# Neighbour product ahead of the aggregation, self product inside attention, layer norm of the gnn in three groups

## The chip, the cores and the metric

One core of one Trainium2 chip runs the kernel. The metric is the device time of one execution in microseconds (us). Before the change three runs took 770.51, 771.01 and 771.20 us, median 771.01. The engines are PE (matrix products, into the eight banks of PSUM), DVE (vector), ACT (scalar), POOL (GpSimd) and SP, which here only issues DMAs. Each engine takes its instructions in the order in which they were written; engines wait for one another by semaphores.

## The reference

1250 nodes of 512 numbers, 40,000 edges sorted by destination.

```python
xn = layernorm(x)
# gnn
agg = segment_sum(xn[src], dst) / max(count, 1)
h   = xn @ w_self.T + agg @ w_neigh.T + bias
gnn = relu(layernorm(h) * gamma + beta)
# linear attention, 8 heads of 64; phi(t) = elu(t @ proj_mat) + 1
q, k, v = split(xn @ w_qkv)
mix = ((phi(q) @ (phi(k).T @ v)) / (phi(q) @ sum(phi(k)))) @ w_proj + b_proj
x = x + gnn + mix
# feed-forward: shared and 8 routed experts (2 of one group of 4 for each node)
y = layernorm(x) * ln_scale + ln_bias
x = x + shared(y) + sum of two weighted expert outputs(y)
```

## The kernel before

All rows live on chip as ten tiles of 125 nodes. Every product with weights is split: both operands are a high and a low float16 half, and three of the four combinations are summed, so that one tile times one 512x512 matrix is 4 x 3 = 12 matmuls (`split3`, L1291). A "unit" is a weight block of 128x2048 floats: SP loads it into one of two staging buffers (L283), ACT writes its high half scaled by 256 (L423), DVE its low half (L733), into one of eight slots.

The stages, in PE's order, are these.

1. Prologue. The rows are normalised by tiles (`stats`, `scale_rows`), transposed (`turn_x`) and split (`xT_high` on ACT, `xT_low` on DVE). Key weights are folded with the projection matrix (`fold`, `wp_high`, `wp_low`). Then come key products (`keys_mm`; ACT's relu and exp, DVE's `key_sum`) and value products (`values_mm`), and their sum over nodes (`kvacc`). Beside it ACT writes the high halves of the rows (`rows_high`) and POOL the low halves (`rows_low`, L339) for the aggregation. DVE then works out from the sorted edges where each block of destinations begins (L830 to L874).
2. Counting and aggregation, 45 rounds. DVE writes one-hot matrices of a round (L885, L888) into a ring of four buffers, PE counts edges by product (L1325) and, one block of 125 destinations later, sums the sources' rows with these counts (`spread`, L1337). Key and value products and folds are put between rounds at fixed places (`KEY_AT`, `VAL_AT`, `FOLD_AT`).
3. Query stage. DVE divides the ten blocks of sums by the counts (L981); PE transposes them (`means_T`, L1481) among the twelve query products, ACT and DVE split them (L562, L985). Query features are relu and exp on ACT, a sum on DVE (L996).
4. Attention. For each tile PE has `att` (16 small products, L1509), `att_turn` of the tile before (four transposes, L1518), and `project` of the one before that (12 matmuls). DVE divides (L1010, L1017), ACT and DVE split the transposed tile (L586, L1022), DVE adds the projection to x (`mix_add`, L1028), POOL has added b_proj (L348). Banks of `att` alternate.
5. gnn. For each tile PE has a bias product (L1302), 12 matmuls of the self weights and 12 of the neighbour weights with the transposed means into one bank. ACT copies it out (L592). DVE has statistics, scale and shift in groups of 4, 4 and 2 tiles (`gnn_norm`), adds to x and norms again (`ffn_norm`), PE transposes the result (`yT`, L1551), ACT applies ln_scale and ln_bias (L600) and both split it (L603, L1097).
6. Hidden layer of the experts, `hid_e`, 48 matmuls a tile in four banks; ACT has silu (L611) and a store (L615), DVE the product (L1106). The `yT` of groups 1 and 2 stand in pairs between halves of tiles. At tile 4 the router's small products stand between the others. Then come the shared layer, the routed experts and the output.

## Time and profile before

| | us |
|---|---|
| median of three runs | 771.01 |
| the profiled execution | 768.86 |
| its span, first to last instruction | 767.0 |
| PE busy in the span | 728.9 (95%) |
| DVE busy | 410.6 (54%) |
| ACT busy | 262.2 (34%) |
| POOL busy | 172.3 (22%) |
| PE's share of the chain of waits | 75% |

The numbers of the last section come from the profiled execution, with times counted from the start of its span. A matmul's own duration in the trace overlaps with the next one, so what a group of matmuls costs is read from the distance between the starts of groups, or from the chain of waits, which gives each piece only its own time.

### The profile page before, as it was taken

The numbers are of one execution on the slowest core, as the hardware profiler recorded it, in microseconds if no ns is written. First come the engines' busy times: TensorE is split into PE (matmuls) and PEld (weight loads), VectorE is DVE, ScalarE is ACT, GpSimd is POOL, SyncE is SP. The second block draws the span as 40 slices with busy tenths as digits, with TensorE's granted clock in tenths as the row PEclk, the third lists the DMA queues.
The fourth block names the chain that finished last, engine by engine and source line by source line (L and its number), as shares of the span: only waits on it lengthen the run. The fifth ranks groups of instructions, "written<-read, shape, count | busy, mean of one in ns | idle before, by whom it ended". The sixth has DMA issues, their size and how long they took to land.

```text
span 767.0 us, 12139 instructions
## 1 busy us (share of the span) xinstructions
PE 728.9 (95%) x4376; PEld 449.7 (59%) x4376; DVE 410.6 (54%) x805; ACT 262.2 (34%) x386; POOL 172.3 (22%) x167
## 2 busy tenths in 40 slices
PE   6989999999799999989999999999889999999998
PEld 5645677776466655656665654445744555555554
DVE  5978977894466768687435432222254524421064
ACT  3852222221483222325634223333353624422000
POOL 3340000000016000002212237742221222211363
PEclk9999999999999999999999999999999999999999
DMA  9200003000021133001144312113167766443675
GB/s 238 97 1 1 1 1 111 1 1 14 1 81 58 56 114 106 1 1 43 47 136 124 93 48 57 43 32 99 51 246 255 279 232 232 128 132 126 201 204 163
DMA packets 24418, 73.91 MB, mean 96 GB/s; under 512 B 7059, under 2 KB 7405, under 8 KB 20274
## 3 DMA queue, kind: packets, MB, share of 16 engines
q1 hardware_dynamic: 8607, 39.74, 15.4%
q0 software_dynamic: 10768, 25.52, 11.5%
q10 hardware_dynamic: 4994, 8.01, 2.9%
q8 instruction: 31, 0.51, 0.3%
q14 instruction: 18, 0.14, 0.1%
HBM read 57.90 MB, written 15.31 MB: 95 GB/s over the span
## 4 chain that ended last, share of the span: by engine, by line
PE 75%; DVE 11%; ACT 6%; issue 3%; DMA 3%; DVEq 0%; POOL 0%; ACTq 0%; SPq 0%; POOLq 0%
PE banks L1295 55%; PE banks L1337 6%; PE banks L1325 6%; PE banks L1638 2%; DMA y_rows<-xT 1%; DVE st L756 1%; ACT W L423 1%; DVE W L733 1%; PE banks L1509 1%; PE banks L1318 1%; DMA x<-in_x 1%; DMA stg<-in_units 1%; PE banks L1518 1%; DVE xn L1106 1%; ACT big L600 1%
## 5 line engine op out<-in xcount | busy, mean ns | idle before, releaser
L1295 PE MATMUL banks<-W,xT 128*125 128x512 f16 (+1 forms) x1392 | 318.0, 383 | 10.0 <-ACT xT L698 4.4
L1295 PEld LDWEIGHTS banks<-W,xT 128*125 128x125 f16 (+2 forms) x1392 | 165.2, 122 | 139.2 <-issue 18.1
L1295 PE MATMUL banks<-xT,W 128*128 128x500 f16 (+1 forms) x720 | 129.8, 342 | 1.8 <-DVE xn L1245 1.4
L1295 PEld LDWEIGHTS banks<-xT,W 128*128 128x128 f16 x720 | 70.3, 98 | 59.5 <-issue 2.8
L733 DVE SCALAR_TENSOR_TENSOR W<-stg,W 128x2048 f16<-128x2048 f32 x30 | 68.2, 2290 | 44.4 <-ACT W L423 44.4
L1295 PE MATMUL banks<-W,big 128*125 128x512 f16 x360 | 81.5, 380 | 0.0
L1295 PEld LDWEIGHTS banks<-W,big 128*125 128x125 f16 x360 | 48.3, 136 | 29.2 <-issue 2.3
L365 POOL DMA_INDIRECT xn<-h_rows,tokidx x29 | 35.4, 1221 | 128.3 <-PE banks L1638 118.5
L1265 DVE CAST xT<-banks 128x1024 f32 x22 | 26.9, 1222 | 69.2 <-PE banks L1638 69.2
L354 POOL TENSOR_TENSOR big<-xn,big 125x512 f16<-125x512 f32 x20 | 23.4, 1172 | 176.4 <-ACT big L615 176.4
L423 ACT ACTIVATE W<-stg 128x2048 f16<-128x2048 f32 x30 | 56.5, 1904 | 3.9 <-DMA stg<-in_units 3.9
L348 POOL TENSOR_TENSOR x<-x,bproj 125x512 f32<-125x512 f32 x10 | 14.4, 1478 | 181.9 <-DVE big L996 181.9
L1337 PE MATMUL banks<-W,big 125*125 125x512 f16 x200 | 54.0, 393 | 0.6 <-ACT big L554 0.6
L1245 DVE SCALAR_TENSOR_TENSOR xn<-banks,xn 128x500 f32<-128x500 f32 (+1 forms) x24 | 14.2, 591 | 69.8 <-ACT xn L677 69.8
L698 ACT ACTIVATE xT<-banks 128x512 f32<-128x512 f32 x23 | 13.7, 596 | 66.8 <-PE banks L1295 50.6
L378 POOL TENSOR_TENSOR big<-xn,big 128x500 f16<-128x500 f32 (+1 forms) x24 | 22.7, 945 | 46.0 <-ACT big L680 46.0
L885 DVE TENSOR_TENSOR W<-big 125x2000 f16<-125x2000 f16 x26 | 31.1, 1197 | 3.3 <-DVE big L880 3.2
L522 ACT ACTIVATE big<-banks 128x500 f16<-128x500 f32 (+1 forms) x27 | 14.2, 527 | 49.2 <-PE banks L1325 49.2
L677 ACT ACTIVATE xn<-banks 128x500 f32<-128x500 f32 (+1 forms) x24 | 12.4, 516 | 52.7 <-PE banks L1295 47.6
L1106 DVE SCALAR_TENSOR_TENSOR xn<-banks,xn 125x512 f32<-125x512 f32 x20 | 13.8, 689 | 30.6 <-ACT xn L611 30.5
L1638 PEld LDWEIGHTS banks<-ident,xn 128*128 (+1 forms) x384 | 24.0, 100 | 8.5 <-issue 1.8
L1638 PE MATMUL banks<-ident,xn 128*128 128x128 f16 x384 | 26.2, 223 | 2.9 <-POOLq L370 1.5
(289 smaller groups left out, 856.1 us busy)
## 6 DMA issues: line engine op xcount, KB each, us to landing
stg<-in_units SPq DMA_DIRECT2D x30, 1024.0 KB
y_rows<-xT ACTq DMA_DIRECT2D x29, 256.0 KB
h_rows<-big POOLq DMA_DIRECT2D x10, 500.0 KB, 3.6
out_x<-x SPq DMA_DIRECT2D x10, 224.0 KB
stg<-in_wqkT SPq DMA_DIRECT2D x2, 1024.0 KB, 11.9
x<-in_x SPq DMA_DIRECT2D x2, 896.0 KB
xn<-h_rows,tokidx POOLq DMA_INDIRECT x29, 4.5
x<-in_x SPq DMA_DIRECT2D x1, 448.0 KB
```

Source lines behind the costliest of these rows:

```text
L354: g.tensor_tensor(hrow[t % 2][:, HID + 512 * u:HID + 512 * (u + 1)], mscr[0:P, 1024 + 512 * u:1536 + 512 * u], hrow[t % 2][:, 512 * u:512 ...
L365: g.indirect_dma_start(hg[i % 2], None, h_rows, bass.IndirectOffsetOnAxis(ap=tokidx[:, i:i + 1], axis=0)).then_inc(g_in[i % 2], 16)
L378: g.tensor_tensor(hT[:, 1, j, c0:c0 + w], mscr[:, 1024 + 512 * (n % 2):1024 + 512 * (n % 2) + w], hT[:, 0, j, c0:c0 + w], ALU.subtract).th ...
L423: s.activation(W[:, u % NSLOT, 0, :], stg[:, u % NSTG, :], ACT.Copy, scale=WS).then_inc(S["w_h"], 1)
L733: v.scalar_tensor_tensor(out=W[:, u % NSLOT, 1, :], in0=stg[:, u % NSTG, :], scalar=WS, in1=W[:, u % NSLOT, 0, :], op0=ALU.mult, op1=ALU.s ...
L885: v.tensor_tensor(oht[z % RING], iotaK.unsqueeze(1).to_broadcast(wide), krel[k].rearrange("p (a b) -> p a b", b=2).unsqueeze(2).to_broadca ...
L1106: v.scalar_tensor_tensor(out=mscr[0:P, 1024 + 512 * u:1536 + 512 * u], in0=ps[2 * u + 1][0:P, :], scalar=HS / WS, in1=mscr[0:P, 512 * u:51 ...
L1265: v.tensor_copy(hgT[:, bass.ds((i + 1) % 2, 1), 1].rearrange("p z j n -> p (z j) n"), turned[1]).then_inc(S["hg_l"], 1)
L1295: ins = te.matmul(dst, lhs(sl, c), rhs(sr, c), start=(first and c == 0 and k == 0), stop=(last and c == n - 1 and k == 2))
L1325: ins = te.matmul(ps[q][:, h * KEYS:(h + 1) * KEYS], ohp[z][:, a, :, b], oht[z][:, a, :, b], start=(a == 0 and b == 0), stop=(a == CH // 2 ...
L1337: ins = te.matmul(ps[4 + z][0:BLK, :], CT[z][0:P, t, :], xs[:, s, t, :], start=(t == 0 and s == 0), stop=(t == TILES - 1 and s == 1))
L1638: ins = te.matmul(turned[s][:, j, :], rows(s * HID + j * 128), ident16[:, :], start=True, stop=True)
```

## The change

The aggregation is linear, so agg @ w_neigh.T is the sum of the rows (xn @ w_neigh.T)[src], divided by the count. The changed kernel computes that product for every source row in the prologue, and the aggregation sums its results.

- w_neigh is no unit any more. SP loads it raw right behind the first two tiles of x (x now comes in groups of 2, 4 and 4 tiles, the key weights behind them); ACT and DVE split it in four pieces each (`wn_high`, `wn_low`). `neigh_mm(t)` is 12 matmuls; ACT (`yn_high`) and DVE (`yn_low`) split its result straight from PSUM into what `spread` reads. `rows_high` and POOL's `rows_low` are gone.
- Five key products and one value product now stand ahead of the rounds, where nine and four stood; the others are between the rounds, at changed places.
- Division, `means_T` and their splits are gone from the query stage. It has two unit conversions and `bias_rows`. POOL's additions of b_proj start at its beginning, where they began after it.
- The self product stands in the attention loop between `att` and `att_turn` of the same tile; its bank and the sums, times the reciprocal count, are combined by DVE (`combine`), with the first statistics. `att` has two banks instead of four.
- The gnn layer norm goes in groups of 3, 3 and 4 tiles, the first of them in the attention loop; the transposes of each group stand together, four in a row. The router's small products are at tile 5.

The core of the diff:

```diff
-KEY_AT = {3: 9}
-VAL_AT = {1: 4, 5: 5, 10: 6, 16: 7, 22: 8, 28: 9}
-FOLD_AT = {12: 4, 15: 5, 18: 6, 21: 7}
+KEY_AT = {1: 5, 4: 6, 7: 7, 10: 8, 13: 9}
+VAL_AT = {2: 1, 5: 2, 8: 3, 11: 4, 16: 5, 20: 6, 24: 7, 28: 8, 32: 9}
+FOLD_AT = {17: 4, 21: 5, 25: 6, 29: 7}
+XG = [(0, 2), (2, 4), (6, 4)]
+LG = [(0, 3), (3, 3), (6, 4)]
...
 # ACT, after the query stage
+            for t in range(TILES):
+                if t == 3:
+                    sqrts(*LG[0])
+                if t == 6:
+                    sqrts(*LG[0])
+                    sqrts(*LG[0])
+                act.wait_ge(S["tT_mm"], t + 1)
...
+                s.activation(attT(t)[:, 0], ps[6 + t % 2][:, 0:C * P]...
+                if t < 3:
+                    unit(U_EIN + t)
+                if t == 7:
+                    for n in range(C):
+                        yT_high(n)
+                if t == 8:
+                    unit(U_EIN + 3)
...
+            hid_e(0)
+            hid_e(1, (0,))
+            sqrts(*LG[1])
+            sqrts(*LG[1])
+            hid_e(1, (1,))
+            for n in range(C, 2 * C):
+                yT_high(n)
+            sqrts(*LG[2])
+            hid_e(2)
+            hid_e(3, (0,))
+            sqrts(*LG[2])
+            sqrts(*LG[2])
+            hid_e(3, (1,))
+            hid_e(4, (0,))
+            for n in range(2 * C, 3 * C):
+                yT_high(n)
+            hid_e(4, (1,))
...
 # DVE
+            def yn_low(t):
+                dve.wait_ge(S["xs_h"], t + 1)
+                v.scalar_tensor_tensor(out=xs[:, 1, t, :], in0=ps[4 + t % 2][0:P, :], scalar=HS / WS, in1=xs[:, 0, t, :], op0=ALU.mult,
+                                       op1=ALU.subtract).then_inc(S["xs_l"], 1)
...
+            def combine(t):
+                dve.wait_ge(S["gn_mm"], t + 1)
+                link(v.scalar_tensor_tensor(out=h[:, t, :], in0=h[:, t, :], scalar=cntacc[:, t:t + 1], in1=ps[2 + t % 2][0:P, :],
+                                            op0=ALU.mult, op1=ALU.add))
+                v.bn_stats(st[:, t, :], h[:, t, :]).then_inc(S["gn_add"], 1)
...
+            for t in range(TILES):
+                att(t)
+                if t >= 2:
+                    mix_add(t - 2)
+                if t < 3:
+                    unit(U_EIN + t)
+                if t == 3:
+                    gnn_rsqrt(*LG[0])
+                if t == 4:
+                    gnn_scale(*LG[0])
+                if t == 5:
+                    ffn_add(*LG[0])
+                if t == 6:
+                    ffn_norm(*LG[0])
+                if t == 8:
+                    for n in range(C):
+                        yT_low(n)
+                if t == 9:
+                    unit(U_EIN + 3)
+                combine(t)
+                attT_low(t)
...
+            ffn_norm(*LG[2])
+            hid_e(3, (1,))
+            late_constants()
+            hid_e(4, (0,))
+            for n in range(2 * C, 3 * C):
+                yT_low(n)
...
 # PE, prologue
             turn_x(0)
             turn_x(1)
+            neigh_mm(0)
+            neigh_mm(1)
+            turn_x(2)
+            turn_x(3)
...
             fold(0, ps[2])
             fold(1, ps[7])
+            neigh_mm(2)
+            turn_x(4)
...
 # PE, attention
+            for t in range(TILES + 1):
+                if t < TILES:
+                    att(t)
+                    self_mm(t)
+                    att_turn(t)
+                if t >= 1:
+                    project(t - 1)
+                if t == 7:
+                    for n in range(C):
+                        if n == 1:
+                            pe.wait_ge(S["tT_rdy"], 8)
+                        yT(n)
...
             hid_e(0)
-            yT(4)
-            yT(5)
-            hid_e(1, (0,))
-            yT(6)
-            yT(7)
-            hid_e(1, (1,))
+            hid_e(1)
+            for n in range(C, 2 * C):
+                yT(n)
             hid_e(2)
...
+            hid_e(3)
+            hid_e(4, (0,))
+            for n in range(2 * C, 3 * C):
+                yT(n)
+            hid_e(4, (1,))
```

## Rows read from the trace of the kernel before

**Rows 1.** Busy time by stretch: length, then each engine, PEclk, DMA share, GB/s.

```profile
0.00:62.66 62.66, 51.77 (x312) 36.61 (x313) 45.63 (x110) 34.58 (x61) 19.93 (x33) 1.00 0.37 103
62.66:188.92 126.26, 123.11 (x935) 89.58 (x934) 101.92 (x214) 29.25 (x53) 0.00 (x0) 1.00 0.06 20
188.92:225.99 37.07, 31.83 (x187) 18.70 (x186) 20.23 (x38) 21.28 (x43) 0.00 (x0) 0.95 0.09 29
225.99:329.62 103.63, 102.24 (x588) 65.47 (x587) 71.96 (x158) 30.99 (x44) 14.40 (x10) 0.98 0.20 67
329.62:378.10 48.48, 44.86 (x217) 28.54 (x218) 31.71 (x85) 24.24 (x40) 10.26 (x10) 1.00 0.12 33
```

**Rows 2.** Waits of PE: total, times, longest.

```profile
PE banks L1481 <- DVE big L985: 5.2, 2, 3.2
```

**Rows 3.** The chain of waits: start, own time, piece.

```profile
93.07 2.59 PE banks L1295 x12
...
206.56 0.86 PE banks L1481 x8
```

**Rows 4.** Timeline of the prologue and first rounds: start, duration, instruction, idle time before.

```profile
15.48 0.69 DVE L777 SCALAR_TENSOR_TENSOR W<-banks,W 128x512 f16<-128x512 f32 x1
...
42.74 0.65 DVE L830 TENSOR_REDUCE big<-big 80x4 f32<-80x500 int32 x1 [2.18 <-issue]
...
44.99 1.06 DVE L836 CAST big<-big 80x4 f32<-80x4 int32 x1
...
46.09 0.19 DVE L837 CAST etabs<-etabs 125x50 f32<-125x50 int32 x1
...
57.19 1.20 DVE L885 TENSOR_TENSOR W<-big 125x2000 f16<-125x2000 f16 x1 [0.49 <-DVE big L880]
...
76.46 1.07 PE L1325 MATMUL banks<-W 125*128 125x250 f16 x8
```

**Rows 5.** Timeline of attention.

```profile
227.89 14.40 POOL L348 TENSOR_TENSOR x<-x,bproj 125x512 f32<-125x512 f32 x10 [181.86 <-DVE big L996]
...
232.01 1.90 ACT L423 ACTIVATE W<-stg 128x2048 f16<-128x2048 f32 x1
...
233.95 2.29 DVE L733 SCALAR_TENSOR_TENSOR W<-stg,W 128x2048 f16<-128x2048 f32 x1 [1.12 <-ACT W L423]
...
243.61 1.09 PE L1509 MATMUL banks<-kvbd,big 64*125 64x65 f32 x16
...
244.97 0.76 DVE L1017 TENSOR_TENSOR xn<-banks,rs 125x256 f32<-125x256 f32 x2
...
247.80 1.09 PE L1509 MATMUL banks<-kvbd,big 64*125 64x65 f32 x16
```

**Rows 6.** Timeline of the gnn products, the bias product of two tiles.

```profile
276.01 0.42 PE L1302 MATMUL banks<-rows,ones 2*125 2x512 f16 x1
...
281.69 0.42 PE L1302 MATMUL banks<-rows,ones 2*125 2x512 f16 x1
```

**Rows 7.** Timeline of the norms of group 0 (four tiles).

```profile
294.91 0.17 DVE L741 TENSOR_SCALAR rs<-mv 125x4 f32<-125x4 f32 x1
...
296.36 2.74 DVE L1067 SCALAR_TENSOR_TENSOR xn<-xn,mv,gcat 125x512 f32<-125x512 f32 x4
...
304.44 2.47 DVE L756 BATCH_NORM_STATS2 st<-x 125x6 f32<-125x512 f32 x4
```

**Rows 8.** Two stretches of 12 and 12 matmuls, and that of the late constants, by engine.

```profile
196.08:200.31 4.23, 4.23 (x15) 1.68 (x13) 0.68 (x1) 0.59 (x1) 0.00 (x0) 0.60 0.00 0
231.49:235.30 3.81, 3.81 (x15) 1.93 (x13) 2.20 (x3) 2.38 (x2) 3.81 (x4) 0.69 0.00 0
271.16:274.01 2.85, 2.85 (x15) 1.82 (x14) 2.67 (x8) 0.00 (x0) 0.00 (x0) 1.00 0.00 0
```

**Rows 9.** Timeline of the hidden layer, ACT.

```profile
338.73 1.28 ACT L611 ACT_TABLE_LOAD   x1
...
344.70 0.75 ACT L600 ACTIVATE big<-banks,lnsb 128x500 f32<-128x500 f32 x1
```

488 lines of the change are left out of this document (200 added, 288 removed).

## The prediction

> **What bounds the kernel now.** I read the summary first: the tensor engine (PE) is busy 95% of the span and is most of the chain of waits, so the question of each edit is what work it takes from PE and what idle time it opens or closes there. I then cut the span at the kernel's own stages [rows 1]. Prologue, first row: PE is busy 51.8 of 62.7 us. Counting and aggregation, second row: 123.1 of 126.3. The query stage, third row: 31.8 of 37.1, with a granted clock of 0.95. Attention and the gnn products, fourth row: 102.2 of 103.6. The hidden layer up to its fifth tile, fifth row: 44.9 of 48.5. The whole edit lies before 378 us; behind it nothing changes but that everything comes earlier or later. The list of waits shows that PE's longest wait inside a stage is for the vector engine (DVE) and its low half of the transposed means, 5.2 us in two waits, one of 3.2 [rows 2].
>
> **Work that is removed.** Ten transposed means leave PE: eight transposes took 0.86 us [rows 3], 40 take 4.3. The neighbour product itself is only moved: 12 matmuls are 2.59 us [rows 3], ten tiles 25.9. The self product, its bias rows and the feed-forward transposes stay.
>
> **Query stage.** Without means nothing stands between the twelve query products. Eight of them are 500 wide (2.54 us each by the same column rate as 2.59 for 512) and four 250 wide (1.3): 25.5 us. ACT needs about 1.45 us for one, so PE keeps the pace. The new attention wants all twelve banks released where it wanted the tenth: about 0.9 us behind the last product. So 26.4 where 37.07 were [rows 1]: 10.7 less, of which 4.3 is the work above and 6.4 idle time, slow clock included (range 5 to 7). What is late next is nothing of this stage; the two unit conversions in it lie beside PE work.
>
> **Prologue and the first rounds.** The neighbour product needs its weight split and x transposed, and its result is evacuated and split: one more ACT step (about 0.6) and one more DVE step (0.69) a tile, by the like split of the folded weights [rows 4]; bounds 0.5, a split from SBUF in a unit, and 0.9. I walk DVE's queue. First rows at about 5.5 (an estimate for half the bytes; anything up to the end of the warm-up matmuls at 12.1, less 4 us of statistics, is hidden), both halves of the weight by 16.0, so the first product starts at 16.0 with 2.8 us of idle PE before it. Then statistics, inverse root and scaling of tiles 2 to 5 (2.5+0.4+1.45+1.9), statistics of tiles 6 to 9 (2.5), two splits of products and two of x: the third product can start at 26.8, PE having run dry at 24.1. Tile 4's start at 34.7 is PE's own pace, and so are the rest: the tenth ends at 52.2, its split at 53.8. There DVE begins the index block, which began at 42.74 [rows 4]: 11.1 later. That block took 14.45 to the first one-hot [rows 4]; it now has one more key sum (0.7) and a wait for PE (0.4). Two tiny casts in it took 0.95 and 1.06 us, while GpSimd was busy with the subtractions that the change drops; I take back 1.7 (bounds 0 and 1.7, from the 0.19 of the like cast right behind, in the same group). So the one-hots of round 0 start at 67.5 and its count at 69.9, against 62.66, where the second stage begins [rows 1]. In the first five rounds DVE sets the pace again: masks and table lie between the one-hots, and the fifth count comes at 86.0 against 76.46 [rows 4]. Up to there PE did three more products and three fewer key-value sums (7.8-1.35 = 6.4), so 3.1 us of the 9.5 is new idle; 0.9 comes back in round 5, where PE waited for DVE and now has a key product to do. From there the rounds are full of PE work as before, with six products more. Net: 2.2 us of idle added (range -2, if the loads come sooner and the pieces fit, to +6).
>
> *What the skill adds.* The Trainium skill (SBUF — State Buffer, "Who interferes with whom") says that GpSimd and DVE share one port pair as an exclusive lock, for casts and for DVE operations with two inputs in SBUF. The long cast agrees. By the rule the 1.7 us is certain; without it the sum would be 1.7 higher. The rule also speaks against the change, which moves GpSimd's ten bias additions beside the query sums; but a unit split with two SBUF inputs took its usual 2.29 us beside those additions [rows 5], and DVE has some 10 us to spare in that stage.
>
> **Attention with the self product.** One tile of attention was 4.19 us of PE (from one group of products to the next) [rows 5]. Half a gnn tile is added: 5.68 us for 24 matmuls and the bias [rows 6], so 2.59 + 0.36 + 0.14 = 3.09. Ten tiles of 7.28 are 72.8, 12 transposes for the layer norm 1.4. Against that stands the order of the queues. For t = 0, 1, 2 ACT converts a unit (1.90 us [rows 5]) behind its evacuation of the transposed attention, and DVE's split of that unit (2.29) stands ahead of combine(t), attT_low(t) and att(t+1), for which PE waits before the next transposes. From the end of PE's att(0): self 3.05, transposes 0.5, evacuation 0.8, unit 1.9, its split 2.3, combine 1.4 (a 0.69 and a 0.68 operation), low half 0.65, att(1) 0.95 (its two products 0.76 [rows 5], reciprocals ahead): 11.6. PE is through with att(1) and self(1) at 7.6. It waits 4.0 us. In the next two tiles the same loop is 8.6 against PE's 7.2: 1.4 each. Then group 0 of the norms: 1.45 for an inverse root, 4.1 for scale and shift of three tiles, 4.0 for add and statistics, 4.9 for the second norm (two roots, three small steps, three scalings of about 0.5) [rows 7]. DVE's base is 3.75 a tile, so it falls behind in t = 4 to 6 and PE waits 1.1 in t = 7. The four transposes at t = 7 share two banks with ACT behind them: 1.2, and 0.15 at the last projection. Sum: 72.8+1.4+6.8+1.1+1.35 = 83.5; walked through, the pieces overlap and it is 82.6. PE's clock fell to 0.60 right behind the 3.2 us wait and to 0.69 near the start of attention [rows 8]; behind the 4.0 us wait I expect the same, most of it in the shadow of the next waits, and none at the start, since dense products now follow att(0) at once: 0.7 more, 83.3. With 25.9 of neighbour product gone from 103.6, 77.7 would be even: 5.5 too many (range 2 to 9; the low end if the unit loop overlaps where I made it serial).
>
> **Hidden layer.** Before, transposes went in pairs between the halves of a tile. Now four stand in a row, twice. Group 1, in time from the start of tile 0: PE ends tile 1 at 20.8. DVE adds group 1 behind tile 0 (12.0 to 16.1), multiplies tile 1's first half at 17.2, and then has the second norm with two roots that ACT must answer, the first behind a table load of 1.28 [rows 9]: rows ready at 23.5. Two transposes, then the third waits for ACT, which has another table load, a silu and its store first: tile 2 starts at 26.8 where 22.2 would do. 4.6 idle. Group 2: rows are ready in time (52.7 against 52.8), but behind the first two transposes stand ACT's table load, silu and store of tile 3, then tile 4's first half, for which DVE first does the late constants (2.85 us [rows 8]), then the affine evacuation of 0.75 [rows 9]. PE goes on at 60.1, 7.3 later, for 1.8 of work: 5.5 idle. Together 10.1 against 4.4 before (48.48 less 4 x 10.37 of products and 2.6 of transposes); with 0.65 of transposes more, 6.35 too many (range 2 to 9). In the second gap PE stands still for 4.7 us, longer than the 3.2 that cost a slow clock [rows 2, 8]; twelve matmuls there took 4.23 instead of 2.54 [rows 8], so 1.7 on top (0 to 3.5 with the first gap and the prologue's). Routing has 32 us of PE cover left where it had 42 and needs 25: nothing.
>
> **Sum.** -4.3 -6.4 +2.2 +5.5 +6.35 +1.7 = +5.05 us. The profiled execution was 768.86 us (span 767.0), so 773.9; the median of the runs is 771.01, 0.28% higher. On that base: 776.
>
> **Rivals.** *A, faster: DVE's queue does not hold up PE in attention and the hidden layer.* One mechanism: the order in which conversion, combine and low half are queued. For it: DVE is busy only 72.0 of 103.6 us there now [rows 1], so that it has room on the average. Against it: the loop is serial, by the order of the code, and each piece has its row. Price: without the 6.8 and 5.7 us and the 1.7 of clock the sum is -9.1, 762; if only the 6.8 fall away, 769. It decides once these two stages have under some 10 us of new waits where I count 15. *B, no change:* the prologue fits (its 2.2 falls away) and the clock costs nothing: +1.2, 772. For it: both are the least certain terms. *C, worse:* the prologue's two dry spells (2.8 and 2.7) each bring a slow clock, the weight lands late, and the hidden layer's first gap too is followed by a slow clock: +3 and +3, 782.
>
> **Chances.** My forecast 0.40 (773 to 779), C 0.15, B 0.17, A 0.28, of which most near 769. A measurement can tell 0.2%, 1.5 us, from no change. A's upper edge and B's lower lie about that bound, so faster 0.30, same 0.16, slower 0.54. Range 764 to 783; the likeliest case alone 773 to 779.
>
> **What would show it.** The query stage at 26 us without a clock dip (else the 10.7 is wrong). First count near 70. In attention, PE waits before its transposes of about 4, 1.4, 1.4 us for DVE at t = 1 to 3. In the hidden layer waits of transposes for ACT, the longest near 4.7, behind it a granted clock below 1. If the attention waits are under 2 us in all, rival A holds; if the first count comes behind 75, rival C.

## The result, and the profile after

The changed kernel takes 789.25 us (median of four runs, 785.72 to 794.09) where the kernel before took 771.11 beside it: ratio 1.0247, 95% interval 1.0194 to 1.0300. Slower, as forecast, but by 18 us where I said 5, and outside the range of 764 to 783. Its profiled execution took 788.64 us, span 786.8.

The same stretches as in [rows 1], from the profile after, in the same columns (the sixth is the whole tail, from the transposes of the first expert rows on; the 164.27 us between the fifth and the sixth are the same in every profile within 0.03):

```profile
0.00:68.10 68.10, 57.38 (x300) 39.64 (x301) 47.94 (x122) 28.92 (x49) 5.76 (x23) 0.97 0.41 110
68.10:218.33 150.23, 147.15 (x1067) 103.48 (x1066) 107.49 (x222) 38.23 (x70) 0.00 (x0) 0.98 0.05 17
218.33:247.12 28.79, 25.55 (x148) 13.93 (x146) 18.56 (x24) 19.40 (x38) 16.15 (x10) 1.00 0.29 92
247.12:332.51 85.39, 79.60 (x462) 51.15 (x463) 60.41 (x141) 20.61 (x28) 0.00 (x0) 0.92 0.15 49
332.51:405.31 72.80, 61.51 (x271) 38.46 (x270) 45.83 (x107) 29.06 (x46) 13.86 (x13) 0.91 0.11 30
569.58:786.80 217.22, 205.85 (x1186) 110.58 (x1186) 82.74 (x74) 63.58 (x61) 57.74 (x48) 0.98 0.58 194
```

Set against the forecast's own path, stage by stage (us). "First count" is PE's first counting product, with which the rounds begin. The forecast's end of the rounds, 217.0, is their end before (188.92) with the moved neighbour product (25.9) and 2.2 of new idle time:

| stretch | forecast | measured | miss |
|---|---|---|---|
| to the first count | 69.9 | 68.10 | -1.8 |
| rounds (to 217.0, less 69.9) | 147.1 | 150.23 | +3.1 |
| query stage | 26.4 | 28.79 | +2.4 |
| attention | 83.3 | 85.39 | +2.1 |
| hidden layer, against before | +8.05 | +13.7 | +5.7 |
| tail (214.05 before) | 0 | 217.22 | +3.2 |
| sum | +5.05 | +19.8 | +14.7 |

(The hidden layer now runs to tile 5 where [rows 1] end at tile 4: 72.80 less one tile of 10.37 is 62.4, against 48.7 from 329.62 to the like product.)

The column to read first is the last but two, the granted clock. It was below 1 in one stage of [rows 1] that matters, 0.95; now it is 0.92 and 0.91 in attention and the hidden layer. Cut at the places where it fell, it is 0.50, the lower of its two levels (1.2 of 2.4 GHz). Such a piece is called a slow stretch here:

```profile
15.68:19.09 3.41, 3.41 (x10) 1.79 (x8) 2.90 (x14) 0.80 (x2) 0.00 (x0) 0.50 1.07 214
77.12:83.95 6.83, 6.83 (x15) 2.67 (x15) 4.49 (x12) 0.00 (x0) 0.00 (x0) 0.50 0.01 1
247.79:254.61 6.82, 6.82 (x24) 3.90 (x22) 0.97 (x4) 0.00 (x0) 0.00 (x0) 0.50 0.00 0
261.44:268.27 6.83, 5.63 (x16) 3.37 (x16) 3.23 (x6) 2.38 (x2) 0.00 (x0) 0.50 0.36 144
357.01:363.84 6.83, 5.96 (x21) 3.63 (x20) 3.08 (x11) 6.39 (x11) 1.71 (x2) 0.50 0.29 76
394.56:401.39 6.83, 4.86 (x15) 3.20 (x16) 2.94 (x5) 5.74 (x9) 1.16 (x1) 0.50 0.17 51
```

PE is busy 33.5 of these 37.6 us and does half as much as it could: at most 16.8 us are lost. The kernel before had two such stretches of 3.4 us up to the same place. And the waits of PE in the whole kernel (total, times, longest), against [rows 2]:

```profile
PE banks L1542 <- ACT xn L572: 7.5, 6, 5.3
PE banks L1297 <- ACT xT L669: 6.2, 3, 4.5
...
PE banks L1542 <- DVE big L1070: 4.9, 2, 3.3
PE banks L1519 <- DVE xn L1005: 4.7, 3, 3.5
PE banks L1508 <- issue: 3.2, 1, 3.2
PE banks L1297 <- DVE W L760: 2.8, 1, 2.8
PE banks L1327 <- DVE W L877: 2.2, 1, 2.2
```

Each wait that I had named is there: L1519 the transposes of attention, L1542 those of the layer norm, L1297 <- L760 the first neighbour product. L1508, the first attention product, was forecast at 0.9 and is 3.2.

### The profile page after: what moved, and what is told of

Read it like the earlier page. It is cut to its first block, busy times and chain, and to the rows that moved or that the text cites. A ratio compares the mean times of both kernels' runs of the same rounds, so it can differ in the third digit from the quotient of the medians.

```text
span 786.8 us, 12045 instructions
## 1 busy us (share of the span) xinstructions
PE 737.1 (94%) x4336; PEld 451.5 (57%) x4336; DVE 417.8 (53%) x814; ACT 255.7 (32%) x372; POOL 160.3 (20%) x157
## 4 chain that ended last, share of the span: by engine, by line
PE 66%; DVE 14%; DMA 8%; ACT 5%; issue 4%; POOL 1%; ACTq 0%; DVEq 0%; SPq 0%; POOLq 0%
PE banks L1297 48%; PE banks L1339 6%; PE banks L1327 6%; DMA xT<-y_rows,sloti 3%; PE banks L1635 2%; DMA y_rows<-xT 2%; DVE W L703 2%; ACT W L416 2%; DMA x<-in_x 1%; DVE st L726 1%; POOL xT L401 1%; DVE x L1058 1%; DMA stg<-in_units 1%; DVE xn L1108 1%; PE banks L1320 1%
## 5 line engine op out<-in xcount | busy, mean ns | idle before, releaser
L1297 PE MATMUL banks<-W,xT 128*125 128x512 f16 (+1 forms) x1512 | 355.2, 390 | 10.3 <-ACT xT L669 6.2
L1297 PEld LDWEIGHTS banks<-W,xT 128*125 128x125 f16 (+2 forms) x1512 | 186.3, 126 | 155.0 <-issue 29.2
L1297 PE MATMUL banks<-xT,W 128*128 128x500 f16 (+1 forms) x720 | 127.4, 339 | 1.8 <-DVE xn L1247 1.4
L1297 PEld LDWEIGHTS banks<-xT,W 128*128 128x128 f16 x720 | 69.9, 97 | 59.2 <-DVE xn L1247 1.6
L347 POOL TENSOR_TENSOR xn<-xn 125x512 f16<-125x512 f32 x20 | 24.2, 1209 | 198.4 <-ACT xn L605 198.4
L341 POOL TENSOR_TENSOR x<-x,bproj 125x512 f32<-125x512 f32 x10 | 16.1, 1648 | 213.2 <-DVE tab L966 213.2
L416 ACT ACTIVATE W<-stg 128x2048 f16<-128x2048 f32 x29 | 54.5, 1901 | 4.5 <-DMA stg<-in_units 4.5
L1297 PE MATMUL banks<-W,big 128*125 128x512 f16 x240 | 53.9, 381 | 0.0
L1297 PEld LDWEIGHTS banks<-W,big 128*125 128x125 f16 x240 | 31.9, 136 | 19.7 <-issue 2.3
L669 ACT ACTIVATE xT<-banks 128x512 f32<-128x512 f32 x23 | 13.7, 596 | 69.0 <-PE banks L1297 51.8
L874 DVE TENSOR_TENSOR W<-big 125x2000 f16<-125x2000 f16 x24 | 28.8, 1199 | 4.0 <-DVE big L869 3.7
L1297 PE MATMUL banks<-W,xn 128*125 128x512 f16 x120 | 29.7, 402 | 0.0
L648 ACT ACTIVATE xn<-banks 128x500 f32<-128x500 f32 (+1 forms) x24 | 12.4, 516 | 52.7 <-PE banks L1297 47.5
```

Of the source, the lines that this page charges most:

```text
L347: g.tensor_tensor(hrow[t % 2][:, HID + 512 * u:HID + 512 * (u + 1)], mscr[0:P, 1024 + 512 * u:1536 + 512 * u], hrow[t % 2][:, 512 * u:512 ...
L416: s.activation(W[:, u % NSLOT, 0, :], stg[:, u % NSTG, :], ACT.Copy, scale=WS).then_inc(S["w_h"], 1)
L874: v.tensor_tensor(oht[z % RING], iotaK.unsqueeze(1).to_broadcast(wide), krel[k].rearrange("p (a b) -> p a b", b=2).unsqueeze(2).to_broadca ...
L1297: ins = te.matmul(dst, lhs(sl, c), rhs(sr, c), start=(first and c == 0 and k == 0), stop=(last and c == n - 1 and k == 2))
```

## The experiments

Two theories were tested. Theory 1, the clock: most of the miss is slow stretches behind dry spells of PE (idle time between its products), each dearer and more frequent than I priced them. Theory 2, the queues: the waits themselves were sized too low. In the table all stages are from one profile each (us). "Slow" lists the lengths of the slow stretches in the rounds, attention and the hidden layer; the tail is the rest from the experts' first turned rows.

| kernel | first count | rounds | query | attention | hidden | tail | slow |
|---|---|---|---|---|---|---|---|
| changed | 68.10 | 150.23 | 28.79 | 85.39 | 72.80 | 217.2 | 6.8 / 6.8, 6.8 / 6.8, 6.8 |
| e9, again | 69.25 | 148.58 | 28.77 | 85.41 | 72.51 | 217.1 | 3.4 / 6.8, 3.4 / 6.8, 6.8 |
| e1 fill | 69.70 | 151.80 | 28.76 | 82.74 | 68.90 | 213.5 | 10.2 / 3.4, 3.4 / none |
| e2 units | 69.27 | 148.59 | 28.77 | 79.02 | 72.49 | 217.5 | 3.4 / 6.8 / 6.8, 6.8 |
| e3 pairs | 72.18 | 150.23 | 28.77 | 82.69 | 62.77 | 218.8 | 6.8 / 3.4, 3.4 / 3.4 |
| e4 adds | 73.74 | 150.22 | 28.24 | 83.07 | 72.81 | 219.4 | 6.8 / 3.4, 3.4 / 6.8, 6.8 |
| e5 bias | 71.11 | 150.23 | 27.30 | 83.39 | 72.87 | 219.7 | 6.8 / 6.8 / 6.8, 10.2 |
| e6 folds | 79.37 | 150.22 | 28.77 | 82.71 | 72.73 | 217.5 | 6.8 / 3.4, 3.4 / 6.8, 6.8 |
| e12 no low | 69.18 | 150.19 | 28.77 | 85.27 | 69.48 | 218.3 | 6.8 / 6.8, 6.8 / 6.8, 6.8 |
| e15 order | 75.55 | 147.08 | 28.76 | 83.84 | 72.75 | 219.2 | none / 6.8, 3.4 / 6.8, 6.8 |
| e7 four | 80.76 | 148.54 | 27.31 | 77.63 | 62.67 | 219.9 | 3.4 / 3.4 / none |
| e10 three | 69.12 | 147.08 | 27.29 | 79.11 | 62.63 | 220.5 | none / 3.4, 3.4 / none |
| e11 + fill | 76.85 | 147.08 | 27.30 | 76.92 | 62.62 | 215.1 | none / none / none |
| e13 banks | 70.67 | 151.77 | 25.62 | 79.51 | 62.63 | 217.4 | 10.2 / 3.4 / none |
| e14 + fill | 72.41 | 147.10 | 25.62 | 79.46 | 62.64 | 214.9 | none / 3.4 / none |
| e16 best | 71.12 | 147.07 | 25.64 | 75.91 | 62.63 | 215.0 | none / none / none |

The column of the rounds is a measurement of the clock by itself. The code of the rounds is the same in all but e11, e14 and e16 (nine idle products there), and the stage takes 147.08 us with no slow stretch, 148.5 to 148.6 with one of 3.4, 150.2 with 6.8, 151.8 with 10.2: 1.5 to 1.7 us for each 3.4. In attention a stretch costs less: e7, e10 and e11 have the same code there and take 77.63, 79.11 and 76.92 us with 3.4, 6.8 and none, so 0.7 to 1.1 for each 3.4.

The tail, whose code no experiment touches, lies between 213.5 and 220.5 us in these profiles. A difference of a few us between two totals is therefore read from the stages.

### e1: products that nobody reads, in the hidden layer's dry spells

`fill(k)` is k products of 512 columns whose result is never used.

```diff
...
             hid_e(1)
+            pe.wait_ge(S["pr_add"], TILES)
+            fill(14)
             for n in range(C, 2 * C):
...
             for n in range(2 * C, 3 * C):
+                if n == 2 * C + 2:
+                    fill(24)
                 yT(n)
```

> The changed kernel with products that nobody reads, put where the tensor engine stands still in the hidden layer: 14 of 512 columns ahead of group 1's transposes (3.0 us in a wait of 3.3) and 24 between group 2's second and third set (5.2 us in a wait of 5.5). The order and the waits of the other engines stay. Theory 1 (the clock: each dry spell is followed by 6.8 us at 1.2 GHz, which costs 3.4 us): both slow stretches of the stage go, and from its first product to tile 5 it takes 66.1 us where the changed kernel took 72.9; the whole is some 6.8 us below the changed kernel, 782. Theory 2 (queues: the waits themselves are what I sized too low, and the clock falls whatever the engine does): the stage stays at 72.9 or is a little longer, and the whole stays near 789.

787.24 us (781.71 to 788.14), ratio 1.0223 (1.0159 to 1.0288). The total alone shows no clear gain over the changed kernel (1.0247). The profile below is of the fastest of the five executions, at a mean clock of 0.985; the other four, 786.29 to 788.14, had 0.978 and have no trace of their own, so where their slow stretches lay is not known. The stage, at a granted clock of 1.00:

```profile
333.00:401.90 68.90, 64.61 (x308) 40.75 (x307) 45.80 (x107) 29.06 (x46) 13.88 (x13) 1.00 0.12 32
```

Both slow stretches are gone and 3.9 us with them, not 6.8: from the last product of tile 1 to the first of tile 2 it is still 7.0 us (7.35 before), around group 2 10.1 (10.5). A slow stretch costs only what PE would have done in it on the path; about half of these lay in the waits. So in this profile theory 1 holds, at 3.9 for two where it had 6.8, and 13.7 less 3.9 is still 9.8 us of waits and transposes, where I had 6.35: theory 2 has a share too.

### e2: the unit conversions behind the low half

```diff
 # ACT, attention loop
-                if t < 3:
-                    unit(U_EIN + t)
+                if 1 <= t <= 3:
+                    unit(U_EIN + t - 1)
...
 # DVE, attention loop
-                if t < 3:
-                    unit(U_EIN + t)
...
                 combine(t)
                 attT_low(t)
+                if 1 <= t <= 3:
+                    unit(U_EIN + t - 1)
```

> The changed kernel with the three unit conversions of the attention loop one tile later on ACT (t = 1 to 3 for 0 to 2) and, on DVE, behind the low half of the transposed attention instead of ahead of the combination. If the serial loop through conversion and split is what holds the tensor engine (the prediction's step): the waits of 3.9, 1.4 and 1.4 us before the transposes shrink under 1 us together, the slow stretch behind the first of them goes (3.4), and the attention stage is 76 to 79 us where it was 85.4; the whole some 7 us below the changed kernel, 782. Rival (DVE has no room in these tiles whatever the order, with 3.75 us of base work and 2.3 of conversion in 7.3): the waits move to t = 2 to 4 and the stage stays at 83 to 85 us.

783.29 us (781.95 to 785.09), ratio 1.0180 (1.0115 to 1.0244). Attention 79.02 instead of 85.4. Its waits:

```profile
PE banks L1508 <- issue: 3.2, 1, 3.2
PE banks L1519 <- DVE xn L1005: 1.2, 2, 0.9
PE banks L1542 <- ACT xn L572: 1.1, 2, 0.6
```

3.5 of the 4.7 us at L1519 and the second slow stretch are gone, 6.4 together. The prediction's mechanism is right: the serial loop is what held PE.

### e3: the transposes in pairs

Group 1's first pair stands between the two banks of tile 2's first half, the second pair behind it; group 2's pairs stand around tile 4's second half; the late constants go ahead of the hidden layer.

> The changed kernel with the feed-forward transposes of groups 1 and 2 taken in pairs with two or more products of the hidden layer between them, as before the change (ACT's and DVE's evacuations follow in the same places), and DVE's late constants ahead of the hidden layer. Theory 1 (four in a row against two banks make the dry spells, and the clock falls behind them): both waits shrink under 1.5 us and both slow stretches go; from the first product to tile 5 some 63 to 65 us where it was 72.9, the whole near 781. Theory 2 (what holds is DVE's norm of a group, not the rhythm of the transposes): the waits for the rows stay (3.3 us ahead of group 1) and one slow stretch with them: 69 us, the whole near 785.

782.12 us (779.52 to 783.12), ratio 1.0152 (1.0085 to 1.0219). The hidden layer is 62.77, ten less, though one wait of 4.8 us for DVE's product came up towards tile 4, because I had put scale and add of group 2 in one piece. With the inverse root moved ahead of tile 2 (e7, e10) the stage still takes 62.6 us: the wait is split into several of 1.6 to 1.8. Four in a row against two banks was the larger fault. Of the ten us a part is the clock, since this profile has 3.4 us of slow stretches in the stage where the changed kernel has 13.7.

### e4 and e5: what holds PE ahead of attention

The core of the two edits:

```diff
 # e4, POOL
-            pool.wait_ge(S["ring_free"], 1)
+            pool.wait_ge(S["q_rdy"], 3 * PAIRS)
 # e5, DVE: bias_rows() behind att(0); PE, self_mm(0)
-                add_bias(d)
-                split3(d, xl(t), unitv(U_SELF), C, False, True)
+                split3(d, xl(t), unitv(U_SELF), C, True, False)
+                pe.wait_ge(S["b_rdy"], 1)
+                te.matmul(d, ones16[0:2, 0:P], rows16[:, :], start=False, stop=True)
```

> The changed kernel with GpSimd's ten bias additions held back until the query sums are done, as before the change. Theory P (the additions slow DVE's query sums and with them the bias rows for which the tensor engine waits): the sums take 0.7 us each where they took up to 2.3, the bias rows are ready some 1.5 to 2 us sooner, and the query stage takes 27 us where it took 28.8; if the wait then falls below what brings the clock down, 3.4 us more. Against that the first projections' additions to x can come late by one or two us in attention. Whole: 784 to 788. Rival (the place of the bias rows in DVE's queue is the cause, not the additions): the stage stays at 28.5 to 29 us, the whole at 789.

> The changed kernel with the bias rows taken out of the end of DVE's query stage: DVE makes them behind its first tile of attention, and the tensor engine adds the bias behind the first self product instead of ahead of it. The first attention product then waits only for the query sums and banks. Theory 1 (the 3.5 us of idle ahead of attention are the wait for the bias rows, and the slow clock behind it comes of that wait): the gap is about 0.9 us, no slow stretch in the first 7 us of attention, whole some 4 to 6 us below the changed kernel. Rival (DVE is late with the query sums too, slowed beside GpSimd's additions, so the wait moves to the transposes of tile 0): the gap shrinks, but a wait of 1 to 2 us stands before those transposes, a slow stretch stays, and the gain is 1 us or less.

e4: 791.5 us (789.59 to 793.54), ratio 1.0270 (1.0205 to 1.0336). e5: 788.64 us (785.15 to 790.89), ratio 1.0229 (1.0179 to 1.0280). In e4 DVE's sums take 0.68 us, most with ACT to wait for; in the changed kernel, beside POOL's additions, up to 1.75:

```profile
222.74 1.55 DVE L982 SCALAR_TENSOR_TENSOR big<-xn 128x500 f32<-128x500 f32 x1 [2.51 <-ACT xn L562]
...
230.27 1.50 DVE L982 SCALAR_TENSOR_TENSOR big<-xn 128x500 f32<-128x500 f32 x1 [1.41 <-ACT xn L562]
232.06 2.98 DVE L703 SCALAR_TENSOR_TENSOR W<-stg,W 128x2048 f16<-128x2048 f32 x1 [0.30 <-ACT W L416]
...
234.97 1.75 DVE L982 SCALAR_TENSOR_TENSOR big<-xn 128x500 f32<-128x500 f32 x1
...
244.50 0.41 DVE L972 TENSOR_SCALAR rows<-gcat 2x512 f16<-2x512 f32 x1
...
246.17 0.74 DVE L975 SCALAR_TENSOR_TENSOR rows<-rows,ident,gcat 2x512 f16<-2x512 f16 x1
```

But the time between the last query product's start and the first of attention falls only from 3.49 us to 2.96: the slowed sums cost 0.5. Moving the bias rows brings it to 2.02, not to the 0.9 that theory 1 had, and a wait of 0.93 us for the rows comes up at the end of the first self product. So of the two, the bias rows' place is the larger cause; they end at 246.9 and attention starts at 247.12. What is left of the gap is the banks (e13). In e5 no slow stretch follows at attention's start; that was luck, since e10 has the same gap and 3.4 us of slow clock behind it. The total shows neither, behind a first count that was 5.6 and 3.0 us later than in the first profile.

### e6: the folds later

The four folded weights, all three engines, one to two neighbour products later.

> The changed kernel with the four folded weights of the prologue made one to two neighbour products later on all three engines. Theory L (their load, now behind the neighbour weight in the queue, lands late: 0.8 us of wait in the changed kernel's profile, 2.8 in three of the four profiles since): no wait for that load, and the first count near 68 in every run, 2 to 3 us sooner than the 69.3 to 73.7 of those profiles. Rival (DVE's own queue sets the first count, and the wait for the load lies in its shadow): the first count stays between 69 and 73, spread as before; the whole within 1.5 us of the changed kernel.

798.07 us (794.43 to 798.82), ratio 1.0356 (1.0303 to 1.0410): both theories wrong, the first count is at 79.37. ACT and DVE stand still in the middle of the transposes, for the first unit (ACT's rows):

```profile
44.64 0.60 ACT L441 ACTIVATE W<-banks 128x512 f16<-128x512 f32 x1 [0.25 <-PE banks L1320]
49.55 1.91 ACT L416 ACTIVATE W<-stg 128x2048 f16<-128x2048 f32 x1 [4.32 <-DMA stg<-in_units]
```

The unit's load goes into the buffer that the folds read, so it starts behind the last fold. The folds had also filled PE's dry spell at 22 us, which is now 4.6 us long (22.01 to 26.56).

### e7: all four together

> The changed kernel with all four mends: unit conversions behind the low half, transposes of the layer norm in pairs (here with the inverse root of group 2 ahead of tile 2, since in the pairs run a wait of 5.0 us for DVE was left in tile 4), bias rows behind attention's first tile, folds later. Theory 1 (the waits and the slow stretches behind them are independent terms, which add up): -6.4 in attention and -10 in the hidden layer as measured one by one, another -3 there for the wait that was left, -4 to -6 ahead of attention, -2 in the prologue: 762 to 767 us, below the kernel before (769 to 771). Theory 2 (the engines are full enough that a wait taken away in one stage comes back in the next): no more than 13 of these 26 us are had, 775 to 778.

781.08 us (779.49 to 783.05), ratio 1.0139 (1.0093 to 1.0186). Slower than either theory had it, but for one reason: the first count is at 80.76, as in e6. Behind it the gains add up. From the first count to the tail it is 480.4 us (561.20 less 80.76), in e9 499.6 (568.81 less 69.25) and in the changed kernel's first profile 501.5: 19 to 21 less, where the terms behind the prologue were expected at 23 to 25.

### e8: the kernel before, with the additions alone moved

```diff
-            pool.wait_ge(S["q_rdy"], 3 * PAIRS)
+            pool.wait_ge(S["ring_free"], 1)
```

> The kernel before with one edit alone: GpSimd's ten bias additions wait for the end of the aggregation instead of the twelve query sums, so that they run beside DVE's work of the query stage. Theory P (additions of GpSimd with two inputs in SBUF slow DVE's operations with two inputs in SBUF): the query sums take 1.1 to 1.6 us where they took 0.68, the additions 1.6 each where they took 1.44, the low halves with one input in PSUM stay at 0.68, and the stage, where the transposed means wait for DVE anyway, takes 0 to 2 us longer. Rival (the longer sums of the changed kernel come of something else in it): the sums stay at 0.68 us, the whole is unchanged.

779.88 us (778.71 to 785.22), ratio 1.0150 (1.0091 to 1.0210): 10 us slower. The query sums stayed at 0.68, since the additions were over before them. What they met were DVE's ten divisions, one operand in SBUF each, which had taken 4.05 us in the kernel before. So theory P was wrong on what would be slowed, and its 0 to 2 us were far too few; the rival's unchanged total was wrong too. DVE, then POOL:

```profile
190.24 13.96 DVE L981 TENSOR_SCALAR big<-big,etabs 125x512 f32<-125x512 f32 x10
```

```profile
190.00 13.91 POOL L348 TENSOR_TENSOR x<-x,bproj 125x512 f32<-125x512 f32 x10 [144.72 <-DVE tab L977]
```

The two run in lockstep, one for one, 1.40 us from start to start; alone the divisions follow each other after 0.40 us, the additions after 1.23 (e4). The transposes of the means wait 11.3 us for DVE, and a slow stretch of 13.65 us lies in and behind that wait, so the stage's 49.4 us in place of 37.07 are lock and clock together. The Trainium skill (SBUF — State Buffer, "Who interferes with whom") calls the port pair of DVE and GpSimd an exclusive lock. The trace agrees in that both engines are held and take turns; but 0.40 and 1.23 would make 1.63, so some 0.2 us of each pair still overlap.

### e9: the changed kernel again

> The changed kernel once more, without an edit, as the control for the runs beside it and for the prologue, whose first count stood at 68.1 us in its own profile and at 69.3 to 73.7 in the profiles of five kernels with the same prologue. If the load of the folded weights sets that (it landed 3 us later there), the first count is again between 68 and 74, with the first fold between 23 and 26.5 and the two moving together; the whole between 785 and 794.

791.64 us (787.97 to 793.59), ratio 1.0304 (1.0271 to 1.0337). The first count, 69.25, and the first fold, 24.62, are where they were expected. Behind the first count it repeats the first profile stage by stage, but for the rounds with their shorter slow stretch.

In attention its slow stretches lie elsewhere. The wait of 3.54 us at 258.58 has none behind it, and 3.4 us of slow clock come at 315.17, among PE's first rows behind these transposes, with no wait above 0.95 us since 262:

```profile
310.69 0.81 PE L1542 MATMUL banks<-ident,big 125*128 125x125 f32 x6
312.02 0.51 PE L1542 MATMUL banks<-ident,big 125*128 125x125 f32 x3 [0.53 <-ACT xn L572]
313.13 0.51 PE L1542 MATMUL banks<-ident,big 125*128 125x125 f32 x3 [0.59 <-ACT xn L572]
313.57 1.09 PE L1508 MATMUL banks<-kvbd,big 64*125 64x65 f32 x16
```

```profile
315.17:318.58 3.41, 3.41 (x9) 1.80 (x8) 2.53 (x6) 1.72 (x3) 0.00 (x0) 0.50 0.01 2
```

e10 has the same at 305.51. So a long wait isn't needed for a slow stretch, and doesn't always bring one.

### e10, e13, e14, e16: adding the mends up

e10 is e2, the pairs (with the inverse root of group 2 ahead of tile 2, as in e7) and e5 together. e13 adds:

```diff
                 if t == 0:
-                    pe.wait_ge(S["q_rel"], 3 * PAIRS)
+                    pe.wait_ge(S["q_rel"], 3 * PAIRS - 2)
...
             def self_mm(t):
+                if t < 2:
+                    pe.wait_ge(S["q_rel"], 3 * PAIRS - 1 + t)
```

e14 adds idle products ahead of the first neighbour product and of the third count; e16 puts the bias rows behind the sixth query sum.

> The four mends without the folds, which made the prologue 8 to 11 us longer in both kernels that had them (the load of the first unit waits for the last fold, and DVE's and ACT's queues wait for the unit in the middle of the transposes). Theory 1 (independent terms): the prologue is back at 68 to 74 us, everything else as in the kernel with four mends, whose first count stood at 80.8: 781 less 7 to 11, so 770 to 774, level with the kernel before. Theory 2 (a wait taken away comes back in the next stage): above 777.

> The three mends, and the first attention products wait for the tenth released bank instead of the twelfth (the first two self products for the eleventh and twelfth): in the kernel with three mends the tensor engine still stood still for 1.9 us ahead of attention, with 3.4 us of slow clock behind it. Theory 1 (that gap is the wait for the last banks, which ACT releases 1.45 us apart): the gap falls to about 0.9 us and the slow stretch at the start of attention goes; 1 to 3 us below the kernel with three mends, 768 to 770. Rival (the gap is the query sums, slowed beside GpSimd's additions): the gap stays at 1.9 us and the time too.

> The same with idle products in the two dry spells of the first 80 us: 9 of 128 columns in fp32 ahead of the first neighbour product (wait 3.1 us) and 9 of 512 columns ahead of the third count (wait 2.4 us); the folds stay in their place. Theory 1 (each dry spell brings a slow stretch, which costs 1.7 to 3.4 us): no slow stretch near 15 and 77 us, the first count 1 to 2 us sooner, 2 to 4 us less in all than its neighbour without idle products: 765 to 767. Rival (DVE's queue sets the first count whatever the clock): no gain up to the first count, and less than 1.5 us in all.

> The kernel with idle products and relaxed banks, with the bias rows made by DVE behind the sixth query sum instead of behind its first attention tile: in the last run the tensor engine waited 2.0 us for them at the end of the first self product, with 3.4 us of slow clock there. If DVE's idle time between the query sums (0.7 to 1.4 us each, seen in the changed kernel's profile) takes up the 2.4 us of bias rows, that wait goes and the slow stretch with it: 2 to 3.5 us less, 765 to 767, faster than the kernel before. Rival (DVE is full in this stage beside GpSimd's additions, so the last sums are late by the same 2 us): a wait of 1 to 2 us before tile 0's transposes instead, and the time stays near 769.

| kernel | us | ratio to the kernel before, 95% |
|---|---|---|
| e10 | 770.93 (768.14 to 774.53) | 1.0033 (1.0011 to 1.0055) |
| e13 | 771.42 (765.39 to 774.30) | 0.9989 (0.9948 to 1.0031) |
| e14 | 768.85 (762.12 to 772.51) | 0.9986 (0.9948 to 1.0023) |
| e16 | 763.38 (761.50 to 766.33) | 0.9917 (0.9881 to 0.9953) |

e10 is 20.7 us below e9, which ran beside it, and stands where theory 1 said. In e13 the gap ahead of attention, from the last query product's start, falls from 2.0 us to 0.34, so that part was the wait for the last banks; but the wait moves on to the end of the first self product, and the total stays within the scatter:

```profile
253.72 0.42 PE L1550 MATMUL banks<-rows,ones 2*125 2x512 f16 x1 [1.84 <-DVE rows L980]
```

e14 has no slow stretch in the rounds (147.10 against 151.77 in e13, which had 10.2 us of it). One profile doesn't show that the idle products did it, but all of them together speak for it: the three with idle products there (e11, e14, e16) have none, and of the thirteen other profiles of this family eleven have one. Ahead of the first neighbour product they gain nothing: the first count stays where it was. Between the medians of e13 and e14 lie 2.6 us, with ranges that overlap, and their ratios are the same: the 765 to 767 that theory 1 had is not shown. e16 closes the last wait: the bias rows fit between the sums, the self product ends without it (attention 75.91 against 79.46 in e14), and no slow stretch is left in its profile from the first count to the experts:

```profile
71.12:218.19 147.07, 145.83 (x1076) 103.67 (x1075) 107.11 (x222) 38.27 (x70) 0.00 (x0) 1.00 0.05 17
218.19:243.83 25.64, 25.55 (x147) 13.95 (x146) 17.79 (x22) 17.60 (x32) 16.14 (x10) 1.00 0.22 65
243.83:319.74 75.91, 73.56 (x462) 48.10 (x463) 61.31 (x142) 22.57 (x35) 0.00 (x0) 1.00 0.20 69
319.74:382.37 62.63, 56.09 (x270) 35.50 (x269) 42.90 (x106) 26.87 (x42) 13.46 (x13) 1.00 0.13 34
```

It is 0.8% faster than the kernel before, and some 26 us faster than the change as made (763.38 against 789.25, measured apart), with the same sums of products.

### e11: a mended prologue with idle products

> The three mends and a mended prologue: folds one to two products later, the first unit's conversion moved behind the last product's split on ACT and DVE, so that nothing waits for its load in the middle; 9 idle fp32 products of 128 columns ahead of the first neighbour product (in its wait of 2.8 us) and 9 idle products of 512 columns ahead of the third count (in its wait of 2.4 us). Theory 1 (the slow stretches at 15, 23 and 77 us come of these dry spells, each costs 1.7 to 3.4 us): the prologue has no or one slow stretch, first count at 65 to 68 us, the second stage 3 us shorter, the whole 763 to 767, faster than the kernel before. Rival (DVE's and the loads' pace set the first count, and the clock costs nothing there): first count at 68 to 71, the whole 768 to 772.

772.73 us (772.02 to 779.25), ratio 1.0075 (1.0046 to 1.0105). Both theories were too low. First count at 76.85: the folds stay wrong in their later place even with the unit out of the way. The rounds had no slow stretch (147.08).

### e12: without GpSimd's subtractions in the hidden layer

> The changed kernel without GpSimd's subtractions in the expert hidden layer: the low halves of its rows are left at zero, so this part of the computation is missing. DVE works alone there. Theory P (DVE's norms of groups 1 and 2 are slowed beside those subtractions, which is why the rows came 3 us later than I reckoned): the four affine operations of group 2 take 0.68 to 0.75 us each where they took 0.9, its rows are ready 2 to 3 us sooner, the first wait behind tile 4's half falls from 1.8 to under 0.5; the hidden layer from the first product to tile 5 takes 70 to 71 us where it was 72.8. Rival (the rows are late because the clock and the first gap shift the whole queue): the operations are shorter but the stage stays within 1 us of 72.8.

788.36 us (784.34 to 790.25), ratio 1.0247 (1.0196 to 1.0299). DVE's scale and add of group 2, in the changed kernel and then here:

```profile
368.77 3.63 DVE L1047 SCALAR_TENSOR_TENSOR big<-big,mv,gcat 125x512 f32<-125x512 f32 x4
...
375.81 3.45 DVE L1058 SCALAR_TENSOR_TENSOR x<-big,x 125x512 f32<-125x512 f32 x4
```

```profile
369.33 2.73 DVE L1049 SCALAR_TENSOR_TENSOR big<-big,mv,gcat 125x512 f32<-125x512 f32 x4
...
375.48 2.49 DVE L1060 SCALAR_TENSOR_TENSOR x<-big,x 125x512 f32<-125x512 f32 x4
```

0.9 and 1.0 us less. The wait of 1.6 us for DVE's rows at tile 4 is gone, and the stage is 69.48 against 72.8 and 72.5 with as much slow clock as there: theory P, 3.0 to 3.3 us of the hidden layer is this contention. The median is 3.3 us below e9's, which ran beside it.

### e15: the order of the loads

> The changed kernel with one edit: the load of the folded weights' source is issued ahead of the last four tiles of x instead of behind them. Theory L (this load, late behind the neighbour weight's, holds the folds, 1 to 3 us, and with them everything up to the first count): the tensor engine doesn't wait for it (0.8 to 2.8 us before), the first count is at 66 to 68 us; the whole some 2 us below the changed kernel's 789 to 792. Rival (then the last four tiles of x are late for DVE's statistics, or DVE's queue sets the pace anyway): the first count stays at 69 to 72.

792.74 us (791.67 to 793.45), ratio 1.0279. The wait for the folds' load is gone, and the third neighbour product now waits 4.1 us, with the first count at 75.55: the last tiles of x are late for DVE. This is the rival's mechanism, and it costs more than the 69 to 72 it said.

## Why the prediction was wrong

- **The direction** was right, and so was the reason: what PE saves in transposes and in the query stage, the serial loops of attention and the hidden layer take back. e2 and e3 take those two away and give 6.4 and 10 us.
- **The step that failed: "so 1.7 on top (0 to 3.5 ...)"** and "0.7 more" in attention. I priced one slow stretch with one group of products [rows 8] and counted 2.4 us for all. There are six in the first 405 us of the first profile, five of them of 6.8 us, and they cost 3.1 us in the rounds (150.23 against 147.08), 3.9 in the hidden layer (e1), up to 1.7 in the tail (one stretch of 6.8 where 3.4 stood before). In attention the stage is 83.8 to 85.4 us with 10.2 or 13.7 us of them and 82.7 to 83.1 with 6.8. I had none in the rounds, where PE waits 2.2 us for the third count, and "none at the start" of attention, where 6.8 us follow the wait of 3.2. For attention's 13.7 us no run gives the whole price; at the rounds' 1.6 for each 3.4 it is 6.4, at the 1.35 between 85.4 and 82.7 it is 5.4 (both estimates). The four terms are then 14 to 15 us, against 2.4. The rest of the miss of 14.7, some 2 to 3 us, is the balance of the points below.
- **Query stage: "about 0.9 us behind the last product"** was 3.2 (3.5 from the start of that product). The banks alone are 2.0 of the 3.5 (e5), and the bias rows, which I put beside PE work, 1.5 more. I had named the twelfth bank and forgotten DVE's queue of sums, two units and bias rows: ACT has read the last bank by 245.5, the bias rows end at 246.9. The rest, 25.55 us of products and no dip of the clock in them, is as said.
- **"The rule also speaks against the change ... DVE has some 10 us to spare":** right in the query stage (0.5 us, e4), by luck of what DVE had left there: in e8 the same additions cost 10. I read one unit split of 2.29 us [rows 5] and took its duration for all; a split in the changed kernel took 2.98. Even there the contention was in the trace, on the other engine: the addition that began 0.06 us behind that split, at 234.01, took 3.36 us where the one ahead of it took 1.27. In [rows 5] ten additions stand in one row of 14.40 us, which hides it. Where it did cost, in the hidden layer (e12, 3 us), I took DVE's durations from [rows 7], a stretch without POOL.
- **Hidden layer:** gap 1 was 7.1 us net where I had 6.0, gap 2 10.3 where I had 7.3. "Rows are ready in time (52.7 ...)" failed: they came 1.8 us behind the half tile. The 4.7 us standstill was 5.3. Of the stage's miss of 5.7 us, 2.2 are the clock (3.9 against 1.7) and 3.5 the waits.
- **Attention:** the first wait was 3.5 us (4.0 forecast), and all were 5.8 where I had 9.2 (6.8, 1.1 and 1.35); the slow clock more than filled the difference.
- **Prologue and rounds:** 68.1 and 86.1 for first and fifth count (69.9 and 86.0) are close to what I walked through. The index block begins at 52.02 (53.8 forecast) and takes 13.79 us to the first one-hot (13.7). The 1.7 us that I took back are had: the two casts of 0.95 and 1.06 us now take 0.18 and 0.17, with GpSimd's subtractions gone:

```profile
53.29 0.18 DVE L823 CAST big<-big 80x51 f32<-80x51 int32 x1
53.51 0.17 DVE L824 CAST big<-big 80x4 f32<-80x4 int32 x1
```

  That the fifth count is on the mark is luck: it comes 18.0 us behind the first, where I had 16.1; without a slow stretch it is 14.8 (e15, 75.55 to 90.38). That the first count comes at 68.1 to 73.7 with the same code goes with the folds' load (first fold at 23.1 to 26.4 us) and the clock. The load alone doesn't set it: e3 and e9 have the first fold at 24.59 and 24.62 and the first count at 72.18 and 69.25, e3 with its slow stretch at 23.7, e9 at 14.8. More the runs don't settle (e15 shows only that loading it sooner is no cure).
- **Tail:** forecast at nothing. Up to 1.7 of the 3.2 us is clock (an estimate, half of the 3.4 us more of slow clock); a wait of 1.6 us, in which PE needs a bank that ACT empties only once a store of expert results has landed, was absent before; it is there in nearly all kernels of this family and gone in e1, e11, e14 and e16. Why is open.
- **Rivals:** C came nearest (its dry spells with slow clock) and was still 7 us short. It added the prologue's two and the hidden layer's first, and its late prologue did not come (68.1); the stretches in the rounds and at attention's start were in no rival. A's price of 762, with the queues out of PE's way, is what e16 reaches (763) with the queues put in another order by hand.

## What to carry to other kernels

In this kernel a dry spell of PE of some 2 us or more often had a second price, the slow clock behind it. Each 3.4 us of it cost 1.5 to 1.7 us where PE was full (the rounds) and 0.7 to 1.4 in attention. Whoever reorders the engines' queues should list the dry spells that the new order makes over the whole kernel, and price the slow clock behind each before the small gains. When a step is moved into a loop, take the serial chain through the other engines' queues (here conversion, split, combination, low half) and put what nobody waits for behind what PE waits for; that order alone was worth 6.4 us (e2). And for work moved on GpSimd, look up what DVE does in that very stretch, by operation, and read both engines' rows one by one.

## What the runs showed of the hardware

- The granted clock fell to 0.50 behind idle spells of PE as short as 1.7 us (the gap ahead of attention in e10) and 2.2 us (the third count), but not always: the same wait of 2.2 us was followed by 10.2, 6.8, 3.4 or 0 us of slow clock in different profiles of the same code. It also fell without one, behind the layer norm's fp32 transposes and 16 small products, with waits of at most 0.6 us among them (e9 at 315.17, e10 at 305.51). The scatter of the changed kernel goes with it: 785.72 us at a mean clock of 0.976, 794.09 at 0.966. It makes a wait's price a range.
- Idle products in the wait took it away in the profiles that have them: in the hidden layer in one (e1), in the rounds in three of three (e11, e14, e16). What follows when they outlast the wait, no run shows.
- DVE and GpSimd can hold each other: ten divisions of DVE, 0.40 us each alone, took 1.40 beside ten additions of GpSimd, which went from 1.23 to 1.40 (e8).
